# Windowed attention, tile by tile: another place for the division, the turning and the products with the values

## The chip, the cores and the metric
The kernel runs on one core of a Trainium2 chip, in one launch. The metric is device time in microseconds (us), the median of several executions; lower is better. PE is the matrix engine (TensorE; PEld its weight loads), DVE the vector engine, ACT the scalar engine, POOL GpSimd, SP the queue that issues the DMAs. All engines run their own instruction streams and wait for each other on semaphores.

## What is computed
A network of two attention blocks with mixture-of-experts and adaptive normalisation (which take the first 590 us and are not touched) and then a stack of six layers, called here the tile stage. On 4 sequences of 512 tokens of width 128, each layer does

```python
qkv = shift_tokens(x) @ Wqkv                      # 16 heads of width 64
q = rotary(l2norm(q) * q_scale); k = rotary(l2norm(k) * k_scale)
# a query in window w (32 tokens) sees windows w-1 and w: 64 keys, masked
attn = softmax(q @ k.T * 8)                       # per head: 32 x 64 for each window
x = x + (attn @ v) @ Wo
x = x + (a * gelu(gate)) @ W2 + b2                # a, gate = split(layernorm(x) @ W1 + b1)
```

All of it is float32; the query and key projections are made of three products of split (high and low) operands.

## The kernel before
**Tiles and slots.** A tile is 128 tokens of one sequence: four windows of 32. There are 6 layers x 4 sequences x 4 tiles = 96 tiles, numbered g, with t = g mod 4 the tile's place in its sequence, b the sequence, n = g div 4. The stage is a software pipeline: in slot g each engine runs, in an order written out by hand in a function `slot` of its block, work on tile g, tile g-1 and tile g-2. Nothing plans this order at run time.

**Tile g.** PE makes six groups of three 128x512 matmuls (`project`) into the two banks of `pj`: queries (c = 0, 1), keys (2, 3), values (4, 5). For queries and keys ACT squares each bank, DVE rotates it (`rotate`, two operations) and sums the squares (`lengths`); ACT and POOL make the inverse root (`inverse_root`, `newton`), POOL adds the two rotated parts (`add_parts`) and scales them (`scaled`). ACT copies values to `Vt` (`copy_v`), and only then can the next tile's `project` use that bank.

**Tile g-1.** PE turns the 16 blocks of queries and keys (`turn`, 8 + 8 transposes of 128x128), ACT copies each four out of `tr` (`take_qk_part`), ACT writes the mask into `sc`, and PE adds the scores on it (`window_scores`: 128 pairs of a 64x32 weight load and a 64-column matmul, in two halves of 64). DVE then takes the maximum and subtracts it (`soft1`).

**Tile g-2.** ACT takes the exponential into `Ex` (128 queries x 16 heads x 64 keys), DVE sums and inverts (`soft2`). PE turns the unnormalised probabilities (`turn_probs`, 8 transposes), ACT copies them to `PT` (`take_probs`), and PE multiplies (`values`, two halves of 64 pairs, probabilities as weights, 64 rows by 32 columns of the array, 64 columns of `V2` moving). `V2` holds the values doubled and laid out by window; SP makes it with 8 or 10 DMAs a tile (`windows`). DVE divides by the sum while it takes the product out of PSUM (`weighted`), PE turns the result back (`turn_out`, 8 transposes), ACT copies it to `oT` (`take_out`).

**Per sequence.** Once in four slots come the product with Wo in two halves (t = 0 and t = 2 of the next sequence), the layer norm (`norm_in` at t = 2, `norm_back` at t = 3), and the feed-forward part: all three `ff_up` with their gelus at t = 0 of the second next sequence, `ff_down` at t = 1. Each gelu group makes ACT load another function table and then load the logarithm's table back.

PE's queue holds its slot in this order: queries of g, (wo or ff_up), turn queries of g-1, keys of g with `turn_probs` between its two halves, `values` first half, turn keys of g-1, `values` second half, first half of the values' projection, first half of the scores, second half of both, `turn_out`.

Of the kernel before, what the change touches and what calls it, by code (L numbers as in the profile page):

```python
# [11 lines left out]
ALU = mybir.AluOpType  # L12
# [3 lines left out]
P = 128  # L16
B = 4
# [85 lines left out]
LOG_EXP = 6  # L103
# [6 lines left out]
def build(nc, ins, out):  # L110
    ctx = ExitStack()
    with ctx:
# [53 lines left out]
        lcur = sb("lcur", [P, 9])  # L166
# [98 lines left out]
        def rows(b):  # L265
# [19 lines left out]
        PT = a.take(PAIRS, P)  # L285
# [3 lines left out]
        V2 = slab[:, 0:G * INNER].rearrange("p (b w f) -> p b w f", b=2, w=G)  # L289
        On = slab[:, G * INNER:(G + 1) * INNER]  # L290
# [17 lines left out]
        ld_q, ld_k, ld_v, ld_wo, ld_ff = sem("ld_q"), sem("ld_k"), sem("ld_v"), sem("ld_wo"), sem("ld_ff")  # L308
# [35 lines left out]
        e_tr, on_ok, on_tr = sem("e_tr"), sem("on_ok"), sem("on_tr")  # L344
        v2_in = (sem("v2_even"), sem("v2_odd"))
        pt_cp, o_mm, o_cp, wo_mm, y_att, xs_f = (
            sem("pt_cp"), sem("o_mm"), sem("o_cp"), sem("wo_mm"), sem("y_att"), sem("xs_f"))
# [5 lines left out]
        lc_ok = sem("lc_ok")  # L353
# [22 lines left out]
        FFB = (oo, tr, oo)  # L376
        WOB = (sc[:, 0], oo[:, 1])
        LD_W = (ld_q, ld_k, ld_v)
        LNB_BANKS = (oo[:, 0], tr[:, 0])
# [13 lines left out]
        class Slot:  # L393
# [5 lines left out]
            def __init__(self, l, b, t):  # L399
                self.l, self.b, self.t = l, b, t  # L400
                self.n = l * B + b
                self.g = self.n * T + t
                first, last = l == 0, l == DEPTH
                self.later = 0 < l < DEPTH
                self.new = not last
                self.c_ = t < 1 and b == 0 if last else not (first and b == 0 and t < 1)
                self.d_ = t < 2 and b == 0 if last else not (first and b == 0 and t < 2)
                self.m1 = None if (first and b < 1) or (last and b > 0) else self.n - 1
                self.m2 = None if first and b < 2 else self.n - 2
                self.l1 = l if b >= 1 else l - 1  # L410
                self.l2 = l if b >= 2 else l - 1
                self.y0, self.y1, self.y2 = ((b - k) % B * S for k in range(3))
                self.ahead = None if last or (b == B - 1 and l == DEPTH - 1) else (b + 1) % B * S
# [9 lines left out]
        TA, TZ, MY, MZ = NTILE - 2, NTILE - 1, NB - 2, NB - 1  # L423
        LAST_FF = {MY: (pj, sc, pj), MZ: (pj, sc, tr)}
        LAST_DOWN = {MY: oo[:, 1], MZ: oo[:, 0]}
        LAST_NORM = (tr[:, 0], tr[:, 1])
# [2010 lines left out]
```

## Time and profile before

| | us |
|---|---|
| runs | 2191.80, 2197.83, 2197.89; median 2197.83 |
| profiled execution: span from its first to its last instruction | 2182.5 |
| profiled execution: its own device time | not on the page; the median lies 15.3 above the span |
| tile stage, first to last `soft1` | 594.9 to 2142.2 |
| busy PE, DVE, ACT, POOL in the span | 92%, 83%, 72%, 53% |

The span is one execution, recorded by the hardware profiler. Matmuls are pipelined and their ends are modelled, so that a busy share of PE is above what it needs; the chain of waits tells better what sets the end. `arena` is one large SBUF tensor that holds most tiles of the stage (`ra`, `Ex`, `PT`, `oT`, `Vt`); `slab` holds `V2` and the divided product; `tr`, `sc`, `oo`, `pj` are the four double banks of PSUM. Nearly all matmuls have line 586, transposes line 589, and ACT's operations line 1924, which are helpers.

### The profile page before, as it was taken

To read this page: it belongs to the slowest core of one execution; us is meant where nothing else is said; L and a number is where in the kernel's file an instruction comes from. 1 tells how busy PE (TensorE), PEld (TensorE's weight loads), DVE (VectorE), ACT (ScalarE), POOL (GpSimd) and SP (SyncE) were. 2 spreads that over 40 slices of the span, in tenths; PEclk is the share of its full clock that TensorE was granted. 3 is DMA by queue.
4 is the path that set the end of the run, shared out by engine and by line. 5 is a ranking of instruction groups with operands and counts; after the bars stand their busy time and mean duration, and the time that the engine had idled before them with its cause. 6 is when DMAs were issued, how large, how long until landed. Compare 5 with 4: busy or idle time off the path is not lost.

```text
span 2182.5 us, 82607 instructions
## 1 busy us (share of the span) xinstructions
PE 2005.7 (92%) x34395; PEld 1457.7 (67%) x34395; DVE 1809.4 (83%) x3751; ACT 1579.9 (72%) x3031; POOL 1167.3 (53%) x1413
## 2 busy tenths in 40 slices
PE   6888899987699999999999999999999999999997
PEld 4666654455577776777777777777767777677775
DVE  7888765678798998888988888988888988888884
ACT  4777753365577887787877788777787878887773
POOL 1112110000577676666776667666667767667761
PEclk9999999998899999999999999999999999999999
DMA  4000001000122232222322223322232322332221
GB/s 114 1 2 2 2 31 59 30 1 30 52 72 68 61 105 69 68 63 71 90 72 75 66 58 95 81 68 66 70 87 71 87 58 58 102 82 62 75 59 40
DMA packets 98196, 132.18 MB, mean 61 GB/s; under 512 B 27900, under 2 KB 42882, under 8 KB 97826
## 3 DMA queue, kind: packets, MB, share of 16 engines
q1 hardware_dynamic: 97826, 126.90, 22.0%
q8 instruction: 275, 4.51, 0.8%
q14 instruction: 95, 0.78, 0.1%
HBM read 28.20 MB, written 1.11 MB: 13 GB/s over the span
## 4 chain that ended last, share of the span: by engine, by line
PE 72%; DVE 13%; issue 6%; ACT 6%; POOL 1%; SPq 1%; DMA 0%; DVEq 0%; POOLq 0%; ACTq 0%
PE oo L586 21%; PE pj L586 19%; PE tr L589 14%; PE sc L586 13%; ACT arena L1924 3%; PE tr L586 2%; DVE arena L1729 2%; DVE xn L1318 2%; DVE arena L1486 1%; PE oo L589 1%; DVE arena L1731 1%; DVE arena L1750 1%; DVE arena L1752 1%; PE sc L589 1%; ACT sc L1924 1%
## 5 line engine op out<-in xcount | busy, mean ns | idle before, releaser
L2345 POOL TENSOR_TENSOR arena<-arena 128x1024 f32<-128x1024 f32 x192 | 456.9, 2380 | 336.9 <-DVE arena L1731 336.9
L1924 ACT ACTIVATE arena<-tr 128x512 f32<-128x512 f32 (+2 forms) x874 | 460.8, 570 | 111.9 <-PE tr L589 109.7
L1924 ACT ACTIVATE arena<-pj 128x512 f32<-128x512 f32 x576 | 341.7, 599 | 189.5 <-PE pj L586 150.4
L589 PE MATMUL tr<-ident,arena 128*128 128x128 f32 x2882 | 413.3, 279 | 25.3 <-DMA beta<-in_L_attn_betas 9.8
L1924 ACT ACTIVATE arena<-arena 128x16 f32<-128x16 f32 (+6 forms) x808 | 362.3, 454 | 98.7 <-DVE arena L1486 74.0
L589 PEld LDWEIGHTS tr<-ident,arena 128*128 128x128 f32 x2882 | 330.6, 141 | 93.4 <-issue 34.5
L2363 POOL TENSOR_TENSOR arena<-arena 128x1024 f32<-128x1024 f32 x192 | 366.7, 1910 | 23.2 <-POOL arena L2356 0.9
L1729 DVE TENSOR_TENSOR arena<-pj,rtab 128x512 f32<-128x512 f32 x384 | 259.8, 677 | 24.8 <-ACT arena L1924 23.4
L586 PE MATMUL oo<-slab,arena 64*32 64x64 f32 (+1 forms) x12416 | 232.1, 228 | 41.0 <-issue 26.4
L1731 DVE TENSOR_TENSOR arena<-pj,rtab 128x512 f32<-128x512 f32 x384 | 261.4, 681 | 0.0
L1737 DVE TENSOR_REDUCE arena<-arena 128x8 f32<-128x512 f32 x384 | 255.6, 677 | 0.0
L586 PEld LDWEIGHTS oo<-slab,arena 64*32 64x32 f32 (+1 forms) x12416 | 158.3, 106 | 123.7 <-issue 94.7
L586 PE MATMUL pj<-w_lo,xs_hi 128*128 128x512 f32 x576 | 227.5, 395 | 0.1
L586 PEld LDWEIGHTS sc<-arena 64*32 64x32 f32 x12288 | 136.0, 105 | 91.0 <-issue 75.0
L586 PE MATMUL sc<-arena 64*32 64x64 f32 x12288 | 171.7, 224 | 6.8 <-issue 5.5
L2312 POOL TENSOR_SCALAR rstd<-mv 128x4 f32<-128x4 f32 x40 | 11.4, 284 | 294.3 <-DVE mv L1312 292.2
L1750 DVE TENSOR_REDUCE arena<-sc 128x16 f32<-128x1024 f32 x96 | 117.2, 1220 | 38.5 <-PE sc L586 38.5
L1770 DVE TENSOR_TENSOR slab<-oo,arena 128x1024 f32<-128x1024 f32 x96 | 117.1, 1220 | 18.3 <-PE oo L586 16.2
L1486 DVE CUSTOM_DVE_ANT_0 arena<-pj,biases 128x128 f32<-128x128 f32 (+3 forms) x214 | 101.1, 486 | 24.3 <-PE pj L586 23.2
L586 PEld LDWEIGHTS pj<-w_lo,xs_hi 128*128 128x128 f32 x576 | 110.1, 191 | 16.4 <-issue 12.2
L1752 DVE TENSOR_TENSOR arena<-sc,arena 128x1024 f32<-128x1024 f32 x96 | 117.5, 1224 | 3.3
L1761 DVE TENSOR_REDUCE arena<-arena 128x16 f32<-128x1024 f32 x96 | 116.3, 1212 | 1.0 <-ACT arena L1924 1.0
(289 smaller groups left out, 3802.5 us busy)
## 6 DMA issues: line engine op xcount, KB each, us to landing
slab<-arena SPq DMA_DIRECT2D x576, 128.0 KB, 2.4
slab<-arena SPq DMA_DIRECT2D x336, 64.0 KB, 2.0
wqkv<-in_L_ffn_Wqkv SPq DMA_DIRECT2D x18, 512.0 KB, 4.2
arena<-gate_mem SPq DMA_DIRECT2D x24, 256.0 KB, 4.3
wo<-in_L_ffn_Wo SPq DMA_DIRECT2D x6, 512.0 KB, 4.2
w<-in_L_ffn_W SPq DMA_DIRECT2D x6, 341.0 KB
YT<-in_L_attn_x SPq DMA_DIRECT2D x4, 256.0 KB, 3.5
arena<-in_L_ffn_W SPq DMA_DIRECT2D x1, 1024.0 KB
```

The costliest lines, as they stand in the source:

```text
L586: return nc.tensor.matmul(o, l, r, start=start, stop=stop, **k)
L589: return nc.tensor.transpose(o, i, ident[0:i.shape[0], 0:i.shape[0]])
L1486: v.tensor_tensor_reduce(out=Ssb[:, n % 4, 0:w], in0=SBANK[n % 3][:, 0:w], in1=bias[:, S - w:S], scale=-1.0, scalar=3e38, op0=ALU.add, op1 ...
L1729: v.tensor_tensor(ra[:, t % 2, k, co].rearrange("p (h u d) -> p h u d", u=2, d=DL // 2), src, tc_.unsqueeze(1).broadcast_to(wide), ALU.mult)
L1731: v.tensor_tensor(rb[:, k, co].rearrange("p (h u d) -> p h u d", u=2, d=DL // 2), src[:, :, ::-1, :], ts_.unsqueeze(1).broadcast_to(wide), ...
L1737: v.tensor_reduce(ss[:, k, hf * PAIRS:(hf + 1) * PAIRS, 0], sq[:, c % 2].rearrange("p (h d) -> p h d", d=DL), AX.X, ALU.add).then_inc(ss_o ...
L1750: v.tensor_reduce(mx, s_v, AX.X, ALU.max).then_inc(mx_ok, 1)
L1752: v.tensor_tensor(Tm.rearrange("p (a u) b -> p u a b", u=2), sc[:, :, :].rearrange("p u (a b) -> p u a b", b=2 * WIN), mx.rearrange("p (u ...
L1770: v.tensor_tensor(On.rearrange("p (a u d) -> p u a d", u=2, d=DL), oo[:, :, :].rearrange("p u (a d) -> p u a d", d=DL), ri.rearrange("p (a ...
L1924: return nc.scalar.activation(o, i, f, **k)
L2345: p_.tensor_tensor(r_, r_, rb[:, k, :], ALU.add).then_inc(sum_ok, 1)
L2363: p_.tensor_tensor(r3, r3, rs[:, k, :].unsqueeze(2).broadcast_to([P, HL, DL]), ALU.mult).then_inc(qk_rdy, 1)
```

## The change
In words, for each tile:

- **Division.** POOL multiplies `Ex` by the inverse sums (`normalise`, 128x1024) before the product; DVE no longer divides after it. `soft2` is now called `sums`.
- **Turning.** DVE transposes the divided probabilities in squares of 32x32 from `Ex` into `PT` (`turn_probs` on DVE, one instruction on 128x1024). PE's `turn_probs` and ACT's two `take_probs` are gone.
- **Products.** `values` now uses the values as weights (32 keys by 64 columns) and the turned probabilities as the moving operand (32 columns): 256 pairs of weight load and matmul in one run instead of 2 x 64, half of them from `Vt`, half from `Vp`. They come out turned in the four banks of `oo` and `tr`, so PE's `turn_out` is gone; `take_out` copies from there.
- **Values copy.** `windows` is one or two DMAs a tile (values shifted by one window) instead of 8 or 10. `copy_v` writes without rearranging.
- **Order.** The product is now one slot later (tile g-3), behind the queries' projection of tile g. The scores are one run of 128 pairs. Both halves of the values' projection come after the scores. The feed-forward part is spread: `ff_up` 0 at t = 1, 1 and 2 at t = 3, `ff_down` at t = 1 a sequence later; `norm_back` moves to t = 0; ACT first copies the layer norm's input out of PSUM (`turned_rows`). At t = 3 both inverse roots wait behind the gelus. The drain after the last slot is rewritten in the same manner, and the load of the feed-forward weights is split in two (`up_weights`, `down_weights`).

The diff, cut to the parts that run in every tile:

```diff
     def windows(g, t):
         sp.wait_ge(v_cp, g * 2 + 2)
         wait(sp, o_mm, g - 1)
+        sp.dma_start(Vp[WIN:P, t % 2, :], Vt[0:P - WIN, t, :]).then_inc(v2_in[t % 2], 16)
+        if t > 0:
+            sp.dma_start(Vp[0:WIN, t % 2, :], Vt[P - WIN:P, t - 1, :]).then_inc(v2_in[t % 2], 16)
...
+    def window_scores(g, t):
+        pe.wait_ge(qk_cp, g * 4 + 4)
+        pe.wait_ge(masked, g + 1)
+        for pr in range(PAIRS):
             for u in range(2):
                 d = slice(u * DL, (u + 1) * DL)
...
                               qT[d, pr, w * WIN:(w + 1) * WIN],
                               kT[d, pr, t * P + w * WIN:t * P + (w + 2) * WIN],
                               start=False, stop=True, skip_group_check=True)
...
+    def values(g):
+        n, t = divmod(g, T)
+        pe.wait_ge(pt_ok, g + 1)
+        pe.wait_ge(v2_in[t % 2], (n * 4 + t + 1) * 16 if t % 2 else (n * 3 + t + 1) * 16)
+        pe.wait_ge(qk_cp, min(g + 2, NTILE) * 4)
+        for pr in range(PAIRS):
+            for j in range(2):
+                for u in range(2):
+                    f = slice((2 * pr + u) * DL, (2 * pr + u + 1) * DL)
+                    for w in range(G):
+                        k_ = slice(w * WIN, (w + 1) * WIN)
+                        v_ = Vt[k_, t, f] if j else Vp[k_, t % 2, f]
+                        last = mm(VBANK[w][u * DL:(u + 1) * DL, pr * WIN:(pr + 1) * WIN], v_,
+                                  PT[k_, 2 * pr + u, j, :], start=(j == 0), stop=(j == 1),
+                                  skip_group_check=True)
+        last.then_inc(o_mm, 1)
...
+    def slot(s_):
+        l, b, t, n, g = s_.l, s_.b, s_.t, s_.n, s_.g
+        m1, m2, m3 = s_.m1, s_.m2, s_.m3
+        def banks_free():
+            if g == 3:
+                pe.wait_ge(y_in, B + 1)
+            if t == 0 and m3 is not None:
+                pe.wait_ge(ff_ev, m3 * FFC + 3)
+            if t == 1 and m1 is not None:
+                pe.wait_ge(y_att, m1 * 2 + 1)
+            if t == 1 and m2 is not None:
+                pe.wait_ge(lnb_out, m2 + 1)
+            if t == 2 and m2 is not None:
+                pe.wait_ge(ff_ev, m2 * FFC + 1)
+            if t == 3 and m1 is not None:
+                pe.wait_ge(y_att, m1 * 2 + 2)
+                pe.wait_ge(lnb_cp, m1 + 1)
+        if b == 0 and t == 0:
+            pe.wait_ge(wl_ok[0], l + 1)
+        if t < 2:
+            pe.wait_ge(xs_l, n * 2 + t + 1)
+        project(g, t, 0)
+        project(g, t, 1)
+        if g > 0:
+            crossing(g, 1)
+        if g >= 3:
+            banks_free()
+            values(g - 3)
+        if b == 0 and t == 0:
+            pe.wait_ge(wl_ok[1], l + 1)
+        project(g, t, 2)
+        if g == 0:
+            crossing(g, 1)
+        project(g, t, 3)
+        crossing(g, 2)
+        if g >= 1:
+            for j in range(2):
+                if g >= 3:
+                    pe.wait_ge(o_cp, (g - 3) * 2 + 1)
+                elif g == 2:
+                    pe.wait_ge(qk_cp, 3 + j)
+                turn(g - 1, t - 1, j)
+        if g >= 3:
+            pe.wait_ge(o_cp, (g - 3) * 2 + 2)
+        if t == 0 and m1 is not None:
+            if b == 1:
+                pe.wait_ge(ld_wo, l * 16 + 16)
+            wo_half(m1, 0)
+        if t == 1 and m3 is not None:
+            if b == 3:
+                pe.wait_ge(ld_w2, l * 48 + 48)
+            ff_down(m3, oo[:, 0])
+        if t == 2 and m1 is not None:
+            wo_half(m1, 1)
+        if t == 3 and m2 is not None:
+            ff_up(m2, 1, oo)
+        if g >= 1:
+            for j in range(2):
+                pe.wait_ge(qk_cp, (g - 1) * 4 + j + 1)
+                turn(g - 1, t - 1, 2 + j)
+        if t == 0 and m2 is not None:
+            norm_back(LNB, oo[:, 1], m2)
+        if g == 1:
+            pe.wait_ge(zeroed, 10)
+        if g >= 1:
+            window_scores(g - 1, (t - 1) % T)
+        if t == 1 and m2 is not None:
+            if b == 2:
+                pe.wait_ge(ld_w1, l * 16 + 16)
+            pe.wait_ge(lnb_out, m2 + 1)
+            if m3 is not None:
+                pe.wait_ge(y_ff, m3 + 2)
+            ff_up(m2, 0, oo)
+        if t == 3 and m2 is not None:
+            pe.wait_ge(ff_ev, m2 * FFC + 2)
+            ff_up(m2, 2, oo)
+        if b == 0 and t == 0:
+            pe.wait_ge(wl_ok[2], l + 1)
+        project(g, t, 4)
+        project(g, t, 5)
+        if t == 2 and m1 is not None:
+            pe.wait_ge(xs_f, m1 + 1)
+            norm_in(LNB, oo[:, 0], xsF)
...
+    def sums(g):
-    def weighted(g):
-        ve.wait_ge(ri_ok, g + 1)
-        wait(ve, on_tr, g * 2)
-        ve.wait_ge(o_mm, g + 1)
-        v.tensor_tensor(On.rearrange("p (a u d) -> p u a d", u=2, d=DL),
-                        oo[:, :, :].rearrange("p u (a d) -> p u a d", d=DL),
-                        ri.rearrange("p (a u) -> p u a", u=2).unsqueeze(3)
-                        .broadcast_to([P, 2, PAIRS, DL]), ALU.mult).then_inc(on_ok, 1)
+    def turn_probs(g):
+        ve.wait_ge(en_ok, g + 1)
+        wait(ve, o_mm, g)
+        v.transpose(PT.rearrange("p h j q -> p (h j q)"), Ex.rearrange("p h k -> p (h k)")
+                    ).then_inc(pt_ok, 1)
...
+        if b == 0 and t == 0:
+            weights_low(l, 1)
+            ve.wait_ge(tab_ok, l * 2 + 1)
+        wait(ve, qk_tr, (g - 2) * 4 + 2)
+        rotate(g, t, 0)
+        rotate(g, t, 1)
+        lengths(g, 0)
+        crossing(g, 1)
+        if g == 0:
+            crossing(g, 2)
+        lengths(g, 1)
+        if g > 0:
+            crossing(g, 2)
+        if g == 0:
+            ve.wait_ge(zeroed, 10)
+        clamp(g, 0)
+        if g >= 2:
+            sums(g - 2)
         if t == 0 and m2 is not None:
+            norm_apply(m2)
+        if b == 0 and t == 0:
+            ve.wait_ge(tab_ok, l * 2 + 2)
+        wait(ve, qk_tr, (g - 2) * 4 + 4)
+        rotate(g, t, 2)
+        if t == 1 and m3 is not None:
+            add_ff(m3, oo[:, 0])
+        if t == 2 and m1 is not None:
+            add_attention(m1, 1)
         if t == 3 and m1 is not None:
+            norm_stats(m1)
+        if b == 0 and t == 0:
+            weights_low(l, 2)
+        rotate(g, t, 3)
+        if t == 3 and m2 is not None:
+            ff_gate(m2, 1, oo)
+        lengths(g, 2)
+        crossing(g, 3)
+        lengths(g, 3)
+        clamp(g, 1)
+        crossing(g, 4)
         if t == 0 and m1 is not None:
+            add_attention(m1, 0)
+        if g >= 2:
+            turn_probs(g - 2)
         if t == 1 and m2 is not None:
+            ff_gate(m2, 0, oo)
+        if t == 3 and m2 is not None:
+            ff_gate(m2, 2, oo)
+        if b == B - 1 and t == 0 and l < DEPTH - 1:
             tables(l + 1)
+        if g >= 1:
             soft1(g - 1)
...
+    def take_out(g, j):
+        t = g % T
+        ac.wait_ge(o_mm, g + 1)
+        src = (tr, oo)[j][:, :, 0:PAIRS * WIN].rearrange("p w (a q) -> p w a q", q=WIN)
+        dst = oT[:, :, t * P:(t + 1) * P].rearrange("p a (w q) -> p w a q", q=WIN)
+        act(dst[:, 2 * (1 - j):2 * (2 - j)], src, ACT.Copy).then_inc(o_cp, 1)
+    def weigh_scores(g):
+        ac.wait_ge(t_sub, g + 1)
+        wait(ac, pt_ok, g)
+        act(Ex, Tm, ACT.Exp, scale=8.0).then_inc(e_exp, 1)
...
+        wait(ac, ss_ok, g * 4 - 1)
+        square(g, 0)
+        wait(ac, ss_ok, g * 4)
+        square(g, 1)
+        if g > 0:
+            crossing(g, 1)
+        if g >= 2:
+            weigh_scores(g - 2)
+        if g >= 3:
+            take_out(g - 3, 0)
+            take_out(g - 3, 1)
+        ac.wait_ge(ss_ok, g * 4 + 1)
+        square(g, 2)
+        if g == 0:
+            crossing(g, 1)
         if layer_end:
             table(g + 1, l + 1, 0)
+        ac.wait_ge(ss_ok, g * 4 + 2)
+        square(g, 3)
+        if t == 3 and m2 is not None:
+            gelu_tables()
+        else:
+            inverse_root(g, 0)
+        if g >= 1:
+            take_qk_part(g - 1, (t - 1) % T, 0)
+            take_qk_part(g - 1, (t - 1) % T, 1)
+            mask(g - 1, (t - 1) % T)
+        if t == 0:
+            wait(ac, pj_mm, n * (6 * T))
+            shifted(xs_hi, YT[:, s_.y0:s_.y0 + S], P, S).then_inc(xs_h, 1)
+        if s_.ahead is not None and t == 2:
             if l > 0 or b == B - 1:
                 ac.wait_ge(y_ff, n + 1 - B + 2)
             ac.wait_ge(pj_mm, n * (6 * T) + 6)
             shifted(xs_hi, YT[:, s_.ahead:s_.ahead + S], 0, P).then_inc(xs_h, 1)
         if s_.later and b == 0 and t == 0:
             weights_high(l, 2)
         if layer_end:
             weights_high(l + 1, 0)
+        if t == 3 and m2 is not None:
+            gelu(m2, 1, oo)
+        if g >= 1:
+            take_qk_part(g - 1, (t - 1) % T, 2)
+            take_qk_part(g - 1, (t - 1) % T, 3)
+        if t == 0 and m2 is not None:
+            norm_end_(m2)
         if t == 2 and m1 is not None:
             ac.wait_ge(y_att, m1 * 2 + 2)
             shifted(xsF, YT[:, s_.y1:s_.y1 + S], 0, S).then_inc(xs_f, 1)
+        if t == 1 and m2 is not None:
+            gelu_tables()
+            gelu(m2, 0, oo)
+            log_exp_tables()
+        if t == 3 and m2 is not None:
+            gelu(m2, 2, oo)
+            log_exp_tables()
+            inverse_root(g, 0)
+        if t != 1:
+            inverse_root(g, 1)
+        wait(ac, o_mm, g - T + 2)
+        copy_v(g, t, 0)
+        copy_v(g, t, 1)
+        if t == 1:
+            inverse_root(g, 1)
         if layer_end:
             weights_high(l + 1, 1)
+        if t == 2 and m1 is not None:
+            turned_rows(m1)
         if layer_end:
             table(g + 1, l + 1, 1)
...
+    def normalise(g):
+        gp.wait_ge(ri_ok, g + 1)
+        p_.tensor_tensor(Ex, Ex, ri.unsqueeze(2).broadcast_to([P, HL, 2 * WIN]), ALU.mult
+                         ).then_inc(en_ok, 1)
...
+        late = t == 3 and s_.m2 is not None
+        layer_end = s_.ahead is not None and b == B - 1 and t == T - 1
+        add_parts(g, t, 0)
+        if g == 1:
+            power(LNA, NORM_AT["D", 3])
+        if layer_end:
+            weights_low(l + 1, 0)
+        if not late:
             newton(g, 0)
+        if g >= 2:
+            normalise(g - 2)
+        if not late:
             scaled(g, t, 0)
+        if t == 3 and s_.m1 is not None:
             power(LNB, s_.m1)
+        if t == 0:
+            low_half(n * 2 + 2, YT[:, s_.y0:s_.y0 + S], P, S)
+        if s_.ahead is not None and t == 2:
+            low_half(n * 2 + 3, YT[:, s_.ahead:s_.ahead + S], 0, P)
+        add_parts(g, t, 1)
+        if g == 0:
+            power(LNA, NORM_AT["D", 2])
+        if late:
+            newton(g, 0)
+            scaled(g, t, 0)
+        newton(g, 1)
```

## Rows read from the trace of the kernel before

**Rows 1.** The page: its first line, busy time by engine, and the instruction queue.
```profile
span 2182.5 us, 82607 instructions
PE 2005.7 (92%) x34395; PEld 1457.7 (67%) x34395; DVE 1809.4 (83%) x3751; ACT 1579.9 (72%) x3031; POOL 1167.3 (53%) x1413
q8 instruction: 275, 4.51, 0.8%
```
**Rows 2.** Chain of waits of the tile stage, shares by engine, tile and line.
```profile
by line: PE oo L586 21.5%; PE pj L586 20.5%; PE tr L589 17.5%; PE sc L586 15.0%; issue 4.5%; ACT arena L1924 3.2%; PE tr L586 2.7%; DVE arena L1729 2.1%; DVE arena L1750 1.7%; DVE arena L1752 1.6%; DVE xn L1318 1.6%; DVE arena L1731 1.5%; A
```
**Rows 3.** Busy time by window, the tile stage: length, PE, PEld, DVE, ACT, POOL, PEclk, DMA.
```profile
594.90:2142.20 1547.30, 1470.85 (x30392) 1111.09 (x30390) 1347.40 (x2244) 1221.54 (x2252) 1073.59 (x1281) 1.00 0.28 74
```
**Rows 4.** Instructions of line 1750, the first DVE operation of `soft1`, once a tile.
```profile
L1750 DVE TENSOR_REDUCE arena<-sc x96: 1207/1224/1226, 594.9 to 2142.2; 128x16 f32<-128x1024 f32 x96
```
**Rows 5.** Timeline of DVE: start, length, instruction; two of line 1750.
```profile
1210.52 1.23 DVE L1750 TENSOR_REDUCE arena<-sc 128x16 f32<-128x1024 f32 x1 [1.00 <-PE sc L586]
...
1231.69 1.21 DVE L1750 TENSOR_REDUCE arena<-sc 128x16 f32<-128x1024 f32 x1
```
**Rows 6.** Chain of waits in order of time, 1196 to 1262: start, length, what.
```profile
1205.20 0.90 issue
...
1207.01 0.70 PE pj L586 x3
...
1210.46 1.02 PE tr L589 x8
...
1239.29 0.79 PE oo L586 x53
```
**Rows 7.** Timeline of PE's weight loads around that issue time.
```profile
1202.60 0.70 PEld L586 LDWEIGHTS oo<-slab,arena 64*32 64x32 f32 x64 [0.94 <-DVE xn L1318]
...
1204.41 0.63 PEld L586 LDWEIGHTS oo<-slab,arena 64*32 64x32 f32 x56 [0.17 <-issue]
...
1206.10 0.15 PEld L586 LDWEIGHTS oo<-slab,arena 64*32 64x32 f32 x8 [1.06 <-issue]
```
**Rows 8.** DMA in 1203.6 to 1206.2: busy tenths in 40 slices of 0.065 us, queue.
```profile
DMA  0090000000000000000000000000000000000000
...
q8 instruction: 1, 0.02, 2.7%
```
**Rows 9.** Timeline of PE's weight loads after the last tile's slot.
```profile
2141.14 0.91 PEld L586 LDWEIGHTS sc<-arena 64*32 64x32 f32 x85 [1.05 <-issue]
...
2147.24 1.56 PEld L586 LDWEIGHTS oo<-slab,arena 64*32 64x32 f32 x128 [0.50 <-issue]
```
**Rows 10.** Waits of PE's weight loads, tile stage: total us, times, longest.
```profile
PEld oo L586 <- issue: 115.0, 367, 2.4
```
**Rows 11.** Groups of PE's weight loads by form, from 600 us: count, busy us, mean ns.
```profile
L586 PEld LDWEIGHTS oo<-slab,arena 64*32 64x32 f32 x12288 | 135.6, 105 | 97.9 <-issue 71.8 <-DVE xn L1318 23.4 <-ACT arena L1924 2.5
...
L586 PEld LDWEIGHTS oo<-hT,w 128*85 128x85 f32 x88 | 13.5, 153 | 14.8 <-issue 12.1
```
**Rows 12.** Groups by form on ACT, DVE and POOL in the tile stage.
```profile
L1924 ACT ACTIVATE sc<-wmask 128x1024 f32<-128x1024 f32 x95 | 97.8, 1029 | 1.1
L1928 ACT ACT_TABLE_LOAD x44 | 56.5, 1283 | 0.8
...
L1770 DVE TENSOR_TENSOR slab<-oo,arena 128x1024 f32<-128x1024 f32 x95 | 115.9, 1220 | 16.6 <-PE oo L586 14.5 <-issue 0.4
...
L2345 POOL TENSOR_TENSOR arena<-arena 128x1024 f32<-128x1024 f32 x188 | 447.5, 2380 | 321.5 <-DVE arena L1731 321.5
L2363 POOL TENSOR_TENSOR arena<-arena 128x1024 f32<-128x1024 f32 x190 | 362.5, 1908 | 23.0 <-POOL arena L2356 0.9
```
**Rows 13.** Timeline of ACT: a square, an inverse root and two copies from PSUM.
```profile
1209.42 0.60 ACT L1924 ACTIVATE arena<-pj 128x512 f32<-128x512 f32 x1
1209.92 0.45 ACT L1924 ACTIVATE arena<-arena 128x16 f32<-128x16 f32 x2
1211.09 1.09 ACT L1924 ACTIVATE arena<-tr 128x512 f32<-128x512 f32 x2 [0.72 <-PE tr L589]
```

More of the change, by code:

```diff
@@ L102 @@
 NMAX = 2 * H0 * T
-LOG_EXP = 6
+LOG_EXP, GELU = 6, 10
 TURNED = 2
@@ L402, in __init__ @@
                 self.g = self.n * T + t
[L403 to L413, printed above, removed]
+                self.later = l > 0
+                self.m1 = self.n - 1 if self.n >= 1 else None
+                self.m2 = self.n - 2 if self.n >= 2 else None
+                self.m3 = self.n - 3 if self.n >= 3 else None
+                self.y0, self.y1, self.y2, self.y3 = ((b - k) % B * S for k in range(4))
+                self.ahead = None if b == B - 1 and l == DEPTH - 1 else (b + 1) % B * S
         def run_slots(slot):
@@ L530, in slot @@
                     qkv_weights(l + 1, 0)
-                if s_.c_:
+                if s_.later and b == 2 and t == 0:
+                    up_weights(l)
+                if g >= 1:
                     windows(g - 1, (t - 1) % T)
@@ L1063, in ff_up, with wo_half, ff_down @@
                 mm(bank[0:w, 1], w1[:, o:o + w], hB).then_inc(w1_mm, 1)
+            def wo_half(m, i):
+                half = slice(i * (S // 2), (i + 1) * (S // 2))
+                for p_ in range(PAIRS):
+                    last = mm(oo[:, i, half], wo[:, p_, :], oT[:, p_, half], start=(p_ == 0),
+                              stop=(p_ == PAIRS - 1))
+                last.then_inc(wo_mm, 1)
+            def ff_down(m, bank):
+                for k, (o, w) in enumerate(CH):
+                    pe.wait_ge(ff_ev, m * FFC + k + 1)
+                    last = mm(bank, w2[0:w, k, :], fa[0:w, k, :], start=(k == 0), stop=(k == FFC - 1))
+                last.then_inc(w2_mm, 1)
@@ L1135, in ff_down @@
-                def ff_down(m):
-                    pe.wait_ge(ff_ev, m * FFC + 3)
-                    for k, (o, w) in enumerate(CH):
-                        last = mm(oo[:, 0], w2[0:w, k, :], fa[0:w, k, :], start=(k == 0), stop=(k == FFC - 1))
-                    last.then_inc(w2_mm, 1)
-                if new:
-                    if b == 0 and t == 0:
-                        pe.wait_ge(wl_ok[0], l + 1)
-                    queries(0)
-                    queries(1)
-                    if g > 0:
-                        crossing(g, 1)
@@ L1263, in drain @@
-                for j in range(2):
-                    pe.wait_ge(qk_cp, TZ * 4 + j + 3)
-                    turn_out(TA, j)
+                pe.wait_ge(v_cp, TZ * 2 + 1)
+                ff_down(MX, LAST_DOWN[MX])
+                window_scores(TZ, T - 1)
+                pe.wait_ge(y_att, MZ * 2 + 1)
+                pe.wait_ge(lnb_out, MY + 1)
+                values(TA)
+                pe.wait_ge(v_cp, TZ * 2 + 2)
+                pe.wait_ge(y_ff, MX + 2)
+                ff_up(MY, 0, LAST_FF[MY][0])
```

536 lines of the change are left out of this document (103 added, 433 removed).

## Prediction

> **What bounds the kernel now.** I read the page first. PE is busy for 92% of the span, DVE for 83% [rows 1]; that leaves open which of them sets the end. The chain of waits decides it: of the tile stage's chain 77.2% are the five PE terms (21.5 + 20.5 + 17.5 + 15.0 + 2.7) and 4.5% are "issue", time in which PE waited for nothing that the profile shows; no other engine's entry is above 3.2% [rows 2]. So PE's list of work sets the pace and what is added to it or taken from it counts. The stage holds 95 intervals in 2142.2 - 594.9 = 1547.3 us [rows 3, 4], 16.3 us a tile and 65.2 us a sequence of four. DVE is busy 1347.4/95 = 14.2 us a tile, ACT 12.9, POOL 11.3, and PE's granted clock is 1.00 throughout (the 2.4 GHz level) [rows 3]. The slot that holds three gelus is the long one: 1231.69 - 1210.52 = 21.2 us [rows 5].
>
> The "issue" time is what I looked at longest, because the change feeds PE twice as many small instructions. In one slot a run of 64 pairs of weight load and matmul starts at 1202.60, eight transposes follow, a second run starts at 1204.41, gets 56 pairs far and stands still for 1.06 us before its last 8 [rows 7]. That is 256 instructions after 1202.60. The page counts 275 packets of 4.51 MB on the instruction queue, 16.4 KB each [rows 1], and PE alone has 2 x 34395 instructions, so about 250 to a packet: a packet is a block of some 256. One such packet moves in this stretch, in the third slice of 0.065 us, hence at 1203.73, for 0.027 x 16 x 2.6 = 1.1 us [rows 8], and PE goes on at 1206.10, 2.4 us after it began and 3.5 us after the sequencer could have asked for it. After the last slot the same happens in a run of scores (1.05 us), and the one dense run of 128 pairs takes 1.56 us, 12.2 ns a pair [rows 9]. So PE eats a block of 256 small instructions in 1.56 us, and a block takes up to 3.5 us to come. Now this hurts little, since runs are 64 pairs long with transposes and projections between; the wait "issue" before the products is 115.0 us in 367 pieces, most of them the hand-over after a matmul, 1.2 us a tile [rows 10], of which I put 0.4 to blocks that were late (about one 1 us gap in three slots, an estimate from the gaps in rows 7 and 9).
>
> The Trainium skill (Runtime: NRT & Kernel Launch, Instruction fetch mechanics) says the same of the block, 256 instructions fetched by the sequencer's own DMA, but holds that crossing one is mostly hidden since dispatch is slower than the refill. By that rule the fetch term below is nothing, which is my first rival. Rows 7 and 9 show dispatch faster than the refill.
>
> **The change, part by part (a tile).**
> - Transposes removed: `turn_probs` and `turn_out`, 2 x 8 at 1.02 us for 8 on the chain [rows 6]: -2.0.
> - Products: two runs of 64 pairs at 0.79 [rows 6] = 1.6 become 256 pairs at 12.2 ns = 3.1: +1.5. Not shown are weights of 64 columns on 32 rows with 32 moving columns. Below: 0.70/64 = 10.9 ns [rows 7], 2.8 in all. Above: a weight load of 64 columns may cost the array twice one of 32 (mean 105 ns for 32 columns, 153 for 85 [rows 11]), 24 ns a pair, 6.2 in all. I take 12.2, since moving columns are halved, and PE, not the array, limited the long run.
> - Blocks that come late: a run of 512 instructions holds two block ends. The second is asked for inside the run and costs in full, between 3.5 - 1.56 = 1.9 us and 2.4 (if the request waits as long as in rows 8, 1.1 us, before its packet moves); I take 2.2. The first costs that only if its block begins inside the run and not during the slow projections ahead, some 3 times in 10: 0.7. The scores, now 256 instructions in one run, hold one end, with keys' transposes ahead: 0.7. Less the 0.4 of now: +3.2. Ends: -0.4 (all hidden) and 3 x 2.4 - 0.4 = +6.8.
> - DVE: the division of 1.22 goes, a transpose of 128x1024 comes. The trace has no DVE transpose; by rows it lies between half the division and the 2.38 of POOL's 128x1024 addition [rows 12]; I take 1.2, so 0. DVE's 14.2 stays below the new slot, so even 2.4 is covered.
> - POOL: one more 128x1024 product with a broadcast, 1.91 as line 2363 (at most 2.38) [rows 12]: 11.3 becomes 13.2, hidden below a slot of 19. It stands before `scaled` and the second `add_parts`; `scaled` is wanted a slot later, the DVE transpose has a whole slot before `values(g-3)`. Cover gone: +1 a tile if slots fall below 14.
> - ACT: two copies out of `tr` less (1.09 [rows 13]), four table loads a sequence as before. Not on the chain now: 0 by itself; its order matters, below.
> - DMAs: 8 or 10 become 1 or 2, no engine's wait names them: 0. If the refill of blocks gains from less traffic it is at most tenths of its 1.1 us. The loads of the feed-forward weights are asked for a slot or more ahead: 0.
>
> Sum: -2.0 + 1.5 + 3.2 = +2.7 a tile, x 96 = +259 us.
>
> **The same from the other side.** The new order closes a loop. PE: projections of queries 1.4 (0.70 each [rows 6]), then the products 3.1 + 2.9 = 6.0. Only then ACT, strictly in order: two `take_out`, two squares (which need the projections behind the products), inverse root, two copies, mask, two copies: 1.1 + 1.2 + 0.5 + 1.1 + 1.0 + 1.1 = 6.0 [rows 12, 13] plus some 0.3 of hand-overs. Only then the scores, 1.6 + 0.7; then the projection of values 0.7 and its copy 0.6, which frees the bank for the next tile. Together 1.4 + 6.0 + 6.3 + 2.3 + 1.3 = 17.3; PE's transposes and Wo products fit in ACT's part. At t = 1 and t = 3 the four table loads of 1.28 [rows 12] and three gelus of about 0.6 (a copy's length) stand in ACT's part of the loop or ahead of the copy of the values: +7 a sequence. 4 x 17.3 + 7 = 76.2 against 65.2: +2.75 a tile, +261 over 95. DVE (14.2) and POOL (13.2) wait in it. The two ways agree.
>
> What lies outside the tile stage stays; the drain has one tile more in flight and loses transposes: 0 to +5, I take 0. From the profiled execution: span 2182.5 + 260 = 2442; the median of the runs is 15.3 above the span, which I take as what lies around it: 2458. The overlap of late blocks with ACT's part of the loop can give a little back, so I forecast 2450.
>
> **Rivals.**
> - Blocks are not late (the skill's rule): -2.0 + 1.5 - 0.4 = -0.9 a tile, -86 us; by the loop 76.2 - 4 x 3.6 = 61.8 a sequence, -81 us. 2115, faster. For it: fewer DMAs, and most block ends now cost nothing. Against it: rows 7 and 9, where dense runs stop. It decides where late blocks add less than 0.5 us a tile. Chance 0.14.
> - Half late: blocks are asked for so early that of a long run only one end costs, and the scores none: 2.2 - 0.4, sum +1.3 a tile, +125: 2325. Chance 0.20.
> - Weights of 64 columns bind: 24 ns a pair. Products 6.2 (+4.6); a block now lasts 3.1 us in them, so that late ones cost some 0.5 there, scores 0.7: sum -2.0 + 4.6 + 0.8 = +3.4, +326: 2525. Chance 0.11. The Trainium skill (TensorE: Matmul & The Clock Gate, Wait — 56ns, not 53.3ns?) gives a floor of about 25 ns from one matmul's start to the next, however small. By that floor this rival would hold; 12.2 ns a pair in rows 9 breaks it for packed tiles.
> - POOL or DVE binds instead (the turn waits for POOL's division): its price hides below a slot of 19 us; counts only in the faster case. Chance 0.02, no change in time, about 2200.
>
> **How the numbers follow.** Forecast case 0.53, own range 2380 to 2540. Faster by over 0.3% (what a measurement of this kernel can tell from no change): 0.14, the first rival. Within 0.3%: 0.03. Slower: 0.83. The range: 2230 leaves the first rival and "POOL binds" out (0.16), 2570 about 0.04; the unknown costs, -3.6 to +3.6 a tile in the block term and +3.1 in the pairs, are in it up to those ends.
>
> **What would show it.** Transposes on line 589 from `slab` gone and those from `arena` a third fewer; products of 32*64 with some 24600 pairs. On the instruction queue 12288 more pairs less 1536 transposes, 21500 instructions, are 84 packets more: about 360. "Issue" ahead of the products at 2.5 us a tile or more, with gaps of 2 us inside runs. ACT in the chain of waits with 20% or more, its pieces between the products and the scores. `soft1` to `soft1` 19 us. Wrong if dense runs of 256 pairs take under 3.5 us, stalls included (then faster), or over 6.5 with no gap in them (then the columns bind).

## The result, and the profile after

| | before | after |
|---|---|---|
| median of the runs (lowest to highest), us | 2195.84 (2191.80 to 2197.89, 4 runs) | 2638.72 (2631.43 to 2656.02, 4 runs) |
| ratio, 95% interval | | 1.2025 [1.198, 1.207] |
| mean granted clock over the span | 0.985 | 0.888 |

The change costs 443 us. The forecast, 2450, had the direction and not the size: 2639 lies above its range (2230 to 2570). A kernel's time is that of its runs within 1.5% of its fastest one; this leaves out one run below, the second of e7.

The page of the changed kernel, which answers to [rows 1]. `PEclk` is PE's granted clock in 40 slices of the span, in tenths of full speed.

```profile
span 2654.2 us, 102595 instructions
PE 2139.4 (81%) x45124; PEld 1585.2 (60%) x45124; DVE 1839.4 (69%) x3751; ACT 1498.4 (56%) x2840; POOL 1348.2 (51%) x1509
...
PEclk9999999988888888888898889888888888988887
...
q8 instruction: 357, 5.85, 0.9%
```

No engine is fuller than before: PE falls from 92% to 81%, DVE from 83% to 69%. Time was added in which engines wait. The instruction queue's 357 packets are those forecast (about 360). The chain of waits of the tile stage (against [rows 2]), the stage by windows ([rows 3]) and the first operation of `soft1` ([rows 4]):

```profile
by line: PE oo L575 23.6%; PE pj L575 23.0%; issue 13.6%; ACT arena L1815 12.2%; PE tr L575 7.0%; PE sc L575 7.0%; PE tr L578 6.2%; ACT L1819 2.3%; ACT sc L1815 1.5%; ACT L1824 1.4%; PE oo L578 0.5%; DVE arena L1633 0.4%; ACT wv_hi L1815 0.
```
```profile
598.30:2597.60 1999.30, 1598.32 (x40793) 1236.08 (x40796) 1377.82 (x2244) 1142.39 (x2066) 1253.40 (x1372) 0.87 0.11 33
```
```profile
L1646 DVE TENSOR_REDUCE arena<-sc x96: 1183/1210/1226, 598.3 to 2597.6; 128x16 f32<-128x1024 f32 x96
```

A tile takes 1999.3/95 = 21.0 us, against 16.3. "Issue" (PE waited for nothing that the profile shows) is 13.6% of the chain, against 4.5%; ACT's entries (lines 1815, 1819, 1824) are 17.4%, against 3.2% for its largest before; and the granted clock is 0.87, against 1.00.

One tile in the chain in order of time (start, length, what; small pieces left out):

```profile
1516.63 1.43 issue
...
1519.76 2.05 issue
...
1522.27 2.86 PE pj L575 x6
1525.13 1.26 PE tr L578 x8
1526.39 3.46 PE oo L575 x16
1529.85 0.45 PE tr L578 x4
1530.32 1.09 ACT arena L1815 x2
1531.42 0.04 issue
1531.46 1.48 PE sc L575 x91
1532.94 1.58 PE pj L575 x6
1534.53 0.44 PE oo L578 x4
1534.96 1.40 PE pj L575 x6
```

The first two rows are stops within the run of 256 products. Behind the run come the keys' six matmuls, 2.86 us at a granted clock of 0.50, the 1.2 GHz level; six take 1.40 here at 1534.96, at 1.00, and 1.39 in the kernel before:

```profile
1522.27:1525.13 2.86, 2.86 (x7) 2.17 (x8) 0.46 (x1) 1.69 (x3) 0.00 (x0) 0.50 0.54 150
```
```profile
1211.49 1.39 PE pj L586 x6
```

(The first row is the changed kernel by windows, its clock the third number from the end; the second is from the chain of the kernel before.) Then come eight transposes and the half product with Wo, 3.46 us, and only then ACT's two copies and the scores. ACT, forecast to fill this middle part without a gap, stands waiting for PE three times in it, 2.9 us in all (its timeline; in brackets the wait; the first row's 5.38 us is for the run of products; one more wait of 0.68 stands in the rows left out):

```profile
1522.37 0.60 ACT L1815 ACTIVATE arena<-tr 128x512 f32<-128x512 f32 x1 [5.38 <-PE tr L575]
1522.86 0.59 ACT L1815 ACTIVATE arena<-oo 128x512 f32<-128x512 f32 x1
1523.94 0.60 ACT L1815 ACTIVATE arena<-pj 128x512 f32<-128x512 f32 x1 [0.49 <-PE pj L575]
...
1530.32 1.09 ACT L1815 ACTIVATE arena<-tr 128x512 f32<-128x512 f32 x2 [1.72 <-PE tr L578]
```

The second stop and the instruction queue: DMA in 1518.2 to 1521.8, slices of 0.09 us.

```profile
DMA  0000000000080000000000000000000000000000
...
q8 instruction: 1, 0.02, 2.2%
```

One packet moves at about 1519.2; PE goes on at 1521.8, 2.6 us later ([rows 8] showed 2.4). The waits of PE's weight loads for "issue" in the stage, against the 115.0 of [rows 10] (the products now go to `oo` and `tr`):

```profile
PEld oo L575 <- issue: 213.0, 380, 3.5
...
PEld tr L575 <- issue: 114.3, 60, 3.8
```

That is 3.4 us a tile for 1.2. The stops can be told from other waits by their place. Number all entries of PE's stream in the trace (matmuls, weight loads and its sequencer's own) in order of time. Idle time of over 0.3 us in front of every 256th of them, counted from the 193rd, comes to 235 us in the changed kernel (137 stops) and to 34 before (43 stops); counted from any other of the 256 places it comes to under 10 us in both. So PE stands still where a block of 256 instructions ends. Of the 96 runs of 256 products 71 hold one stop of over 0.3 us and 25 hold two; a run takes 5.6 us on average, of which 2.3 are stops, and the rest makes 12.8 ns a pair. Last, the same instruction at either clock: the projections' matmuls of the stage by form, before and after (count, busy us, mean ns).

```profile
L586 PE MATMUL pj<-w_lo,xs_hi 128*128 128x512 f32 x564 | 221.9, 393 | 0.1
...
L586 PE MATMUL pj<-wk_hi,xs_hi 128*128 128x512 f32 x188 | 95.3, 507 | 13.7 <-DVE arena L1731 13.7
...
L586 PE MATMUL pj<-wk_hi,xs_lo 128*128 128x512 f32 x188 | 74.2, 395 | 0.0
```
```profile
L575 PE MATMUL pj<-w_lo,xs_hi 128*128 128x512 f32 x566 | 261.3, 462 | 3.1 <-issue 3.1
...
L575 PE MATMUL pj<-wk_hi,xs_hi 128*128 128x512 f32 x188 | 123.4, 656 | 4.9 <-issue 3.6 <-DVE arena L1627 1.3
L575 PE MATMUL pj<-wk_hi,xs_lo 128*128 128x512 f32 x188 | 109.5, 583 | 0.0
```

The keys' projections, right behind the long run, pay most (395 to 583 ns). Over all seven forms of projection the busy time rises from 721.2 to 830.1 us.

### The profile page after: what moved, and what is told of

Read it like the earlier page. It is cut to its first block, busy times and chain, and to the rows that moved or that the text cites. A ratio compares the mean times of both kernels' runs of the same rounds, so it can differ in the third digit from the quotient of the medians.

```text
span 2654.2 us, 102595 instructions
## 1 busy us (share of the span) xinstructions
PE 2139.4 (81%) x45124; PEld 1585.2 (60%) x45124; DVE 1839.4 (69%) x3751; ACT 1498.4 (56%) x2840; POOL 1348.2 (51%) x1509
## 4 chain that ended last, share of the span: by engine, by line
PE 65%; ACT 15%; issue 13%; DVE 6%; POOL 0%; SPq 0%; DMA 0%; DVEq 0%; POOLq 0%; ACTq 0%
PE oo L575 23%; PE pj L575 22%; ACT arena L1815 10%; PE sc L575 7%; PE tr L578 6%; PE tr L575 6%; ACT L1819 2%; DVE arena L1382 1%; ACT sc L1815 1%; PE oo L578 1%; ACT L1824 1%; PE sc L578 1%; DVE arena L1392 1%; DVE xn L1214 0%; DVE arena L1633 0%
## 5 line engine op out<-in xcount | busy, mean ns | idle before, releaser
L1815 ACT ACTIVATE arena<-tr 128x512 f32<-128x512 f32 (+2 forms) x586 | 308.6, 554 | 490.9 <-PE tr L575 368.2
L578 PE MATMUL tr<-ident,arena 128*128 128x128 f32 x2126 | 355.4, 307 | 24.4 <-DMA beta<-in_L_attn_betas 9.8
L575 PE MATMUL oo<-arena 32*64 32x32 f32 (+1 forms) x6944 | 312.4, 243 | 67.6 <-issue 60.3
L575 PE MATMUL tr<-arena 32*64 32x32 f32 x6144 | 284.1, 237 | 71.6 <-issue 71.6
L575 PE MATMUL tr<-arena,slab 32*64 32x32 f32 x6144 | 277.5, 237 | 47.5 <-issue 47.5
L575 PE MATMUL oo<-arena,slab 32*64 32x32 f32 x6144 | 273.8, 235 | 46.1 <-issue 46.0
L575 PEld LDWEIGHTS oo<-arena 32*64 32x64 f32 (+1 forms) x6944 | 252.8, 141 | 75.9 <-issue 69.9
L575 PEld LDWEIGHTS oo<-arena,slab 32*64 32x64 f32 x6144 | 243.6, 140 | 87.9 <-issue 87.2
L575 PEld LDWEIGHTS tr<-arena 32*64 32x64 f32 x6144 | 232.6, 144 | 67.1 <-issue 67.1
L575 PEld LDWEIGHTS tr<-arena,slab 32*64 32x64 f32 x6144 | 233.4, 141 | 53.3 <-issue 53.3
```

The costliest lines, as they stand in the source:

```text
L575: return nc.tensor.matmul(o, l, r, start=start, stop=stop, **k)
L578: return nc.tensor.transpose(o, i, ident[0:i.shape[0], 0:i.shape[0]])
L1815: return nc.scalar.activation(o, i, f, **k)
```

## Experiments

Each is a kernel with one edit, timed beside the kernel before on the same chip (2195 to 2199 us there). Ratios are to that, with their intervals.

**Half of the pairs (e1).** The product loop with `for j in range(1, 2)` and `start=True`: the keys of the previous window are left out of the product.

> The changed kernel with only the own window's half of the products (128 pairs instead of 256 a tile; the previous window's half is left out). Late-blocks theory: the products' run, 5.3 us from first to last matmul of which 2.6 us stands still, falls to about 1.3 + 1.2 = 2.5 us; the granted clock of the stage goes from 0.87 back above 0.95, since nothing stands still for 2 us and more; a slot loses 2.8 us directly and some 0.7 by the clock: about 2639 - 96 x 3.5 = 2300 us. Rival, the order's loop (PE's Wo product and transposes, then ACT's copies, then the scores, one after the other) sets the slot whatever the products cost: only the pairs' own 1.3 us goes: 2510 us. Rival, weights of 64 columns bind the array: no gap left or right, 2.7 us of pairs halved, 2500 us.

2265.01 us, 1.0314 [1.0284, 1.0344]. 128 pairs, 128 instructions of either kind less, are worth 374 us, 30 ns a pair, where 12.2 was their own price. The stops at block ends fall from 235 to 49 us. "Late blocks" comes nearest, with 2300; the loop with its 2510 falls as the main cause.

**The run cut up (e2).** The same 256 pairs, in three runs; on ACT the two `take_out` move behind the third square, since the products end later:

```diff
 project(g, t, 0)
+values(g - 3, range(0, 2))
 project(g, t, 1)
-values(g - 3)
+values(g - 3, range(2, 4))
 project(g, t, 2)
+values(g - 3, range(4, 8))
```

> The changed kernel with the run of 256 product pairs cut in three: 64 pairs behind the first query projection, 64 behind the second, 128 behind the first key projection; ACT takes the products out behind the third square instead of ahead of it. Same instructions, same work. Late-blocks theory: projections of 0.7 us between the runs give each block 1.4 us more to come; the time that products stand still falls from 2.6 to about 1.5 us a tile, the clock rises to 0.92: about 2639 - 96 x 1.6 = 2485 us. Rival, the order's loop: the products end as late as before in the slot, so no change, 2620 to 2650 us, and the take-out behind the square costs up to 0.6 us a slot, 2690 us.

2458.97 us, 1.1197 [1.1121, 1.1273]: 180 us less with every instruction still there. So a large part of what the pairs cost lies in the length of their run. The stops at block ends fall from 235 to 71 us, nearly the whole gain, and the clock recovers:

```profile
700.00:2100.00 1400.00, 1196.25 (x31541) 882.29 (x31539) 1067.30 (x1754) 882.93 (x1610) 975.43 (x1065) 0.95 0.13 37
```
```profile
PEld oo L575 <- issue: 258.8, 710, 3.6
```

Of the changed kernel the same window has 0.87, and its waits over the span are 265.6 for `oo` and 127.9 for `tr`, here 258.8 and 40.2.

**The kernel before with 256 pairs (e3), and with its runs joined (e4).** e3 makes each product in two of 32 columns; e4 moves the second half of the products ahead of the keys' transposes and joins the scores' halves.

```diff
-last = mm(oo[q, u, pr * DL:(pr + 1) * DL], PT[d, pr, q], V2[...])
+for h in range(2):
+    c = slice(pr * DL + h * 32, pr * DL + h * 32 + 32)
+    last = mm(oo[q, u, c], PT[d, pr, q], V2[d, t % 2, w, c])
```

> The kernel before with each product matmul of 64 columns made as two of 32 columns, each with its own weight load: 256 pairs a tile, in two runs of 128, nothing else changed and the result the same. Late-blocks theory: +128 pairs at 10.6 ns = 1.4 us, and one block end more a tile, in runs dense enough to pay 1.5 to 2.2 us: +3.2 us a tile, 2196 + 300 = 2500 us, with 50 packets... more exactly 96 more blocks on the instruction queue, and a clock below 1.00 in the stage. Rival, blocks come in time and it is the new order that costs: +1.4 us a tile at most, 2330 us, clock 1.00.

> The kernel before with its runs joined: both halves of the products in one run of 128 pairs ahead of the keys' transposes, both halves of the scores in one run of 128 pairs behind the values' projections. Same instructions, other order. Late-blocks theory: runs of 256 instructions hold one block end each and pay it more often: 0.4 us a tile becomes about 1.2, 2196 + 75 = 2270 us, part of it the order itself. Rival, blocks come in time: within 1% of 2196 us but for the order.

e3: 2546.57 us, 1.1596 [1.1552, 1.164]. e4: 2224.98 us, 1.0132 [1.01, 1.0163]. The old order with nothing but 128 more pairs loses 351 us, nearly what e1 gave back. The number of short instructions is the main cost, in either order. In e3 the stops at block ends rise from 34 to 212 us, which with 150 us for 128 pairs of 12.2 ns is 328 of the 351. Joining runs of the old length costs 29 us, under half of what was expected of it.

```profile
PEld oo L586 <- issue: 280.1, 623, 3.1
...
PEld sc L586 <- issue: 166.2, 300, 2.4
```

These were 163.9 and 87.1 over the span of the kernel before. The scores' own instructions did not change: part of the price falls on the neighbours. All "issue" waits of weight loads together: 403 us before, 617 in e3, 644 in the changed kernel, 541 in e2, 433 in e1.

**The values' projection earlier (e5), and with the short runs (e6).**

```diff
+project(g, t, 4)
+project(g, t, 5)
 window_scores(g - 1, (t - 1) % T)
 ...
-project(g, t, 4)
-project(g, t, 5)
```

On ACT `copy_v` moves behind the last `take_qk_part`.

> The changed kernel with the values' projection (its two halves) on PE ahead of the scores instead of behind them, ACT's copy of the values right behind the last copy of the keys, and inverse_root(1) behind the gelus. The sums are the same. In the trace of the changed kernel the stretch from the end of the scores over this projection and its copy to the next tile's first projection is about 3.9 us of the tile's 21. Theory (the order on the engines costs, beside the late blocks): that tail shrinks by 1.5 to 2 us per tile and some of it comes back ahead of the scores, so 2470 to 2540 us. Rival (only late instruction blocks and the clock decide, the order is free): 2639 within 1%, since the number of instructions is the same.

> The kernel of the run e2_short_runs (product runs of 64, 64 and 128 pairs between the projections) with the order of e5_early_values. If the two costs add, 2459 less what e5 saves (100 to 170 us): 2290 to 2360. If both take away the same waiting time, it is within 2% of the better of the two (2410 to 2459).

e5: 2496.64 us, 1.1365 [1.1344, 1.1386]; e6: 2399.53 us, 1.0923 [1.0891, 1.0954], the best of the changed design with all its work. The order alone is worth 142 us, at about the same granted clock (0.895, changed kernel 0.888) and with nearly the same stops at block ends (219 us for 235), and PE's projections wait less for "issue" (161.2 to 79.6 us). e6 adds only 59 to e2: the two savings overlap by more than half.

**POOL nearly free of the division (e7).** `Ex[:, :, 0:1]` instead of `Ex` in `normalise`: the other 63 keys of each head stay undivided.

> The changed kernel with POOL's division done on one of the 64 keys of each head only (16 of 1024 columns), the rest left undivided, so that POOL is nearly free of it. Theory (POOL lies beside PE and ACT, as its zero in the prediction's sum says): 2639 within 0.5% (2625 to 2652). Rival (the division or DVE's turn behind it ends late and PE's products wait for it): faster by its length where it binds, 2450 to 2580.

2623.08 us, one run. That is 16 us, 0.6%, under the changed kernel's median and 8 under its lowest run (2631). The division took POOL 1.90 us a tile and takes 0.23 here, some 160 us of POOL's time; at most a tenth of that lay on the path. One run can't tell 16 us from nothing.

**The kernel before with quarter runs (e8).**

> The kernel before with its 128 products of a tile issued as four runs of 32, set between the key transposes and the fourth projection, instead of its two runs. Theory (late instruction blocks cost only where a run of short products outlasts the next block's load): the stops of the kernel before, some 54 us over the whole, shrink, and it is 1 to 2% faster, 2155 to 2180 us. Rival (the stops are hidden by other waits already, and later products hold DVE and ACT): within 0.5% or slower, 2190 to 2240.

2210.25 us, 1.0059 [1.0046, 1.0073], in 5 runs: the rival's side. The stops at block ends did not fall (34 us before, 35 here, counted as above; the 54 of the expectation is another count). Cutting runs of 64 further saves nothing.

**Both at once (e9).** e1 with the order of e5.

> Both edits, half of the product pairs (the previous window's keys left out) and the values' projection ahead of the scores. The first alone took 374 us off the changed kernel, the second alone 142. Theory (the pairs with their late blocks and the order on the engines are two costs that add): 2265 less 142, some 2120 us, 3% under the kernel before, with the granted clock at 0.95 to 0.96. Rival (both take away the same waits of PE, and DVE, 80% busy with half of the pairs, sets the rest): 2200 to 2260.

2250.46 us, 1.0246 [1.0221, 1.0272]: the rival. The order that was worth 142 us with 256 pairs is worth 15 with 128. Its waits show why:

```profile
PEld pj L575 <- DVE arena L1627: 227.5, 251, 4.3
```

DVE (82% busy over the span) now frees the bank of the projections late. The stops at block ends are down to 22 us, and it still is slower than the kernel before with half of the product left out; its granted clock is 0.936. In the stage the clock falls to its lower level 50 times, and 40 times the longest stop of PE just before is a wait for DVE's line 1627; in the changed kernel it falls 107 times, 90 of them after an "issue" stop. So a low clock does not need late blocks: waits of PE for DVE do it too.

**What the transposes are worth (e10, e11), and the changed work in the old order (e12).** e10 makes 2 of 8 transposes of the probabilities a tile, e11 also 2 of 8 of the outputs, with ACT's copies cut alike (old rows are used for the rest); e12 is e11 with the pairs of e3.

```diff
-for u in range(4):
+for u in (range(4) if g == 0 else range(3, 4)):      # outputs: g < 4
     pr = 4 * j + u
     last = tp(tr[:, j, u * P:(u + 1) * P], Ex[:, 2 * pr:2 * pr + 2, :])
```

> The kernel before with a quarter of the transposes of the probabilities (two of eight per tile, and ACT's copies cut to a quarter), the products then made from old rows; the first tile keeps all eight. This prices the prediction's term of 2.0 us per tile for the transposes. If they lie on PE's path in full, three quarters of it go: 1.5 us by 96 tiles, 2197 less 144, some 2050 us. Rival (DVE, 83% busy, and ACT's chain bind as soon as PE is shorter): 2110 to 2180, so the term was worth less than half of what the sum gave it.

> The kernel before with a quarter of both kinds of transposes (probabilities and outputs: 4 of 16 a tile, ACT's four copies cut to a quarter), the rest of the products' input and of Wo's input being old rows; the first tiles keep all. The 8 transposes were 1.02 us on the chain, so the 6 left out in e10 stand for 0.77 us a tile, 73 us, and 35 were measured; here 12 go, 1.53 us a tile, 147 us. If the prediction's term holds: 2050. If the half seen in e10 holds: some 2130. Rival (DVE, 83% busy, binds): 2150 or more.

> The same, and each product in two of 32 columns (256 pairs a tile, as in e3_before_pairs): PE then has about the work of the changed kernel in the order of the kernel before. Theory (the changed kernel's order costs over 100 us beside the pairs and the late blocks): 2547 less 60 to 147, so 2400 to 2490, well under the 2639 of the changed kernel. Rival (the order is free, pairs and late blocks alone make the changed kernel's time): 2600 or more.

The expectation of e10 put the transposes' price too high: 6 transposes of 16 stand for 0.77 us a tile, 73 us, as that of e11 says. e10: 2164.60 us, 0.9847 [0.983, 0.9864], 35 us less. e11: 2134.66 us, 0.9718 [0.9691, 0.9746], 63 us less, where the chain of waits promised 147. e12: 2483.08 us, 1.1292 [1.1252, 1.1333]: the pairs again cost 348 us, and the changed kernel is 156 above a kernel of about its work in the old order. Of these 156 only some 21 are stops at block ends (235 us against 215). The chain of e11, by engine:

```profile
PE 65%; DVE 16%; issue 8%; ACT 8%; POOL 1%; SPq 1%; DMA 1%; DVEq 0%; POOLq 0%; ACTq 0%
```

PE was 72% before and DVE 13%: of what PE gave up, others took the larger part.

## Why the prediction failed

By its own terms, in us over the 96 tiles:

| term | forecast | runs |
|---|---|---|
| transposes gone | -192 | -83 (63 for 12 of 16, scaled) |
| 128 more pairs and late blocks | +144 and +307 = +451 | +348 to +374 (e12 less e11; e3; changed kernel less e1) |
| the order, with the clock | 0 | the rest of 443: +152 to +178; 142 come back in e5 |
| DVE, POOL | 0 | POOL 16 at most (e7); DVE not tried |

The loop, in us from one run of products to the next, averaged over 94 slots of PE's timeline. The slots t = 0 and t = 2 hold no gelu; `all` has the four kinds, with 7 us of table loads and gelus a sequence in the forecast:

| part | forecast | t = 0, 2 | all |
|---|---|---|---|
| queries | 1.4 | 1.5 | 1.6 |
| products | 6.0 | 5.6 | 5.5 |
| end of products to scores | 6.3 | 9.3 | 8.9 |
| scores | 2.3 | 1.5 | 1.6 |
| end of scores to next queries | 1.3 | 1.9 | 3.5 |
| sum | 17.3 (19.1 with gelus) | 19.8 | 21.1 |

What failed is the third row, the order and the clock, which the sum had at nothing; the first row was mis-sized as well.

- **Transposes.** The step "2 x 8 at 1.02 us for 8 on the chain: -2.0" was mis-sized: 43% of it was real. A share of the chain says what a piece held, not what its removal gives: in e11's chain DVE, ACT and "issue" have grown. The rival "POOL or DVE binds" named one of these engines, but as a thing of the faster case alone and with no price.
- **Pairs and late blocks.** Right in kind, and for the products nearly in size: dense runs of short instructions stop at block ends, up to 3.8 us at a time, as rows 7 to 9 said. The run took 5.6 us (forecast 6.0) with stops of 2.3 (2.9), and a second stop in 25 of 96 runs, where I had "3 times in 10". The term was too large by the scores' block end, 0.7 a tile: their run takes 1.6 us, 128 pairs at 12.2 ns, and waits for "issue" only 7.7 us in the whole stage. By this late blocks add 2.0 a tile; by the stops at block ends, (235 - 34)/96 = 2.1; by the runs, with 1.5 for the pairs, 2.1 to 2.4 (e3 and e12 keep the scores' two halves). I took 3.2. That is nearer to the rival "half late" (1.8, the scores at none), whose 2325 was missed because it shared the two wrong terms beside it. "Blocks are not late" is out by e2, e3 and the 235 us of stops at block ends, and the Trainium skill's rule with it (Runtime: NRT & Kernel Launch, Instruction fetch mechanics, which calls the crossing mostly hidden): the trace doesn't agree, with waits for "issue" up by 241 us (403 to 644).
- **Weights of 64 columns.** Not the bound: without its stops the run takes 12.8 ns a pair, not 24, and cutting the same pairs into runs gave 180 us back.
- **The loop.** This is the step that failed: "PE's transposes and Wo products fit in ACT's part". They don't. From the end of the products to the scores the tile above takes 1531.46 - 1522.27 = 9.2 us, forecast 6.3, with ACT waiting for PE: keys 2.86, transposes 1.26, Wo half 3.46, transposes 0.45, copies 1.09. I had added ACT's list and never PE's. With the keys at 1.39, as at full clock, the same list is still 7.7. The table shows that it is so in the mean: this part is 3.0 us too long in the slots without gelus while products and scores together are 1.2 shorter than forecast. That the two ways agreed on +2.7 was luck: the sum had the order at nothing and the loop had ACT's list alone. Forecast for the slot 19; it took 21.0.
- **The clock.** This is the second step: both ways used PE's durations at 1.00 throughout. At 0.87 the projections alone were busy for 109 us more. The keys' six matmuls stand on the chain right behind the stops and took 2.8 us in the mean for 1.39, about half of what the loop's middle part is too long. The Trainium skill (TensorE: Matmul & The Clock Gate, What's actually happening) says that the clock falls when PE has idled; its section "Loop structure matters more than you think" ties it to long waits between matmuls, though there for DMAs. The trace agrees: 0.87 with long stops, 0.95 with the same work in shorter runs (e2), 0.94 where PE waited for DVE (e9).
- **ACT, DVE's turn, DMAs.** About as forecast: the transpose took 1.235 us (I took 1.2), the issue waits 3.4 us a tile (I said 2.5 or more), a run of products 5.6 us (I said 3.5 to 6.5), DMAs 0% of the chain. ACT has 17% of the stage's chain, where I said 20 or more.
- **Around the span.** Of the 15.3 us added to the span, only 1.8 lie around it (2656.02 for a span of 2654.2); the rest was scatter between executions (the span of 2182.5 with 1.8 around it is 2184.3, under the lowest of the four runs). It made the forecast nearer, not further.

What stays open: how the some 135 us between e12 and the changed kernel that are not stops at block ends divide between order and clock. e5 gives 142 at the same clock, but the same projections at the old durations would also give some 109; both can't be on the path in full. Nor does e12 share all of the changed kernel's design: its runs are of 128 pairs, and it keeps 4 of 16 transposes, DVE's division and the old copies of the values. No run changed the clock alone, and none tells whether the last 4 of 16 transposes are worth as much as the first 12.

## What to carry to other kernels

Count the instructions of the bounding engine before the columns that they work on: doubling 128 pairs of small products to 256 cost 348 to 374 us here, some 29 ns a pair, when a pair in a dense run shows 12.2. Where they can't be fewer, cut a run of 256 pairs into shorter ones between long matmuls (180 us here; cutting runs of 64 gave nothing). When an order closes a loop over two engines, add up both engines' lists between the same two points. Price a removal by what the next engine allows, not by its share of the chain.

## What the runs showed that was not expected

- Leaving out 12 of the kernel's 16 turning transposes a tile gave 63 us; leaving out 128 of 256 pairs gave 374. The instructions that look small in the groups (a weight load of 140 ns and a matmul of 240, almost wholly overlapped) were the dear ones.
- PE's busy share did not tell its granted clock: e5 (84% busy) had 0.895, e6, the same instructions in shorter runs (85%), 0.956, e9 with a quarter fewer (85%) 0.936.
- The stops for instructions come at block ends by their place alone: 137 of them, 235 us, at every 256th instruction of PE's stream in the changed kernel. Cutting the long run (e2) left 71 us of them, two runs of 128 in the old order (e3) had 212.
- DVE transposes 128x1024 in squares of 32 in 1.235 us, about what its division of the same size took before (1.22):

```profile
L1665 DVE STREAM_TRANSPOSE arena<-arena x96: 1233/1235/1246, 610.6 to 2610.6; 128x1024 f32<-128x1024 f32 x96
```
